# A staggered start of attention, and VectorE's preparation ahead of a wait

## The reference

```
h = token_mixer(x)                       # conv, layer norm, feed forward, max-pool: 748 rows remain
h = h + recurrence(layernorm(h))
h = h + experts_2_of_8(layernorm(h))     # routed, plus a shared one
n = layernorm(h)
q, k, v = n @ W_qkv + b                  # 8 heads of 16
q', k' = relu(q), relu(k), each times cos and times sin of the position
h = h + (causal linear attention of q', k', v) @ W_out + b_out
n = layernorm(h)                         # for the last, routed layer:
logits = conv3(gelu(conv3(n)));  shared = conv1(silu(conv9(n)))
h = h + layernorm(n + experts_2_of_10(n, logits) + shared)
```

## Time and profile before

| | us |
|---|---|
| median of 3 runs | 1531.79 |
| lowest and highest | 1531.74, 1535.3 |
| the profiled execution | 1544.43 |
| its span, first to last instruction | 1542.6 |
| busy in it: PE, VectorE, ScalarE, GpSimd | 1305.9, 1003.6, 644.9, 699.3 |
| mean granted PE clock, as a share of 2.4 GHz | 0.92 |

### The profile page before, as it was taken

How to read it: one execution, slowest core, us unless ns; L and a number is a source line. 1 busy time by engine, 2 the same in 40 slices (tenths; PEclk the granted TensorE clock), 3 DMA queues, 4 the chain that set the end, 5 groups by cost and what they waited for, 6 DMA issues and landing times.

```text
span 1542.6 us, 33397 instructions
## 1 busy us (share of the span) xinstructions
PE 1305.9 (85%) x10360; PEld 1103.2 (72%) x10361; DVE 1003.6 (65%) x3235; ACT 644.9 (42%) x1610; POOL 699.3 (45%) x1055
## 2 busy tenths in 40 slices
PE   6696777787899937778899899988998989999974
PEld 3464646564899935556788778876887989999953
DVE  4467768665466656757863786467663628989946
ACT  1346272523122204335335453445334436666623
POOL 0112556444688853133531444242614526777732
PEclk9697989898999978989999899999998999999987
DMA  6000400003588840010010001000100237777725
GB/s 191 4 21 6 111 27 22 25 21 95 161 266 256 263 170 1 2 42 1 24 61 0 2 14 58 14 1 1 43 1 8 95 97 191 196 194 198 196 88 161
DMA packets 102202, 128.46 MB, mean 83 GB/s; under 512 B 21015, under 2 KB 61181, under 8 KB 101842
## 3 DMA queue, kind: packets, MB, share of 16 engines
q1 hardware_dynamic: 88786, 102.36, 23.1%
q0 software_dynamic: 13312, 24.74, 4.8%
HBM read 96.13 MB, written 34.94 MB: 85 GB/s over the span
## 4 chain that ended last, share of the span: by engine, by line
PE 60%; DVE 15%; issue 7%; DVEq 6%; POOL 5%; ACT 4%; DMA 2%; POOLq 0%; SPq 0%; ACTq 0%
PE psum L980 12%; PE psum L1133 11%; PE psum L989 9%; DVE work L1554 3%; PE psum L1142 3%; PE psum L1047 2%; POOL rows_in L2130 2%; PE psum L1094 2%; PE psum L1072 2%; PE psum L794 2%; PE psum L1191 2%; PE psum L969 2%; PE psum L1018 2%; DVE stats L1537 2%; PE psum L1067 1%
## 5 line engine op out<-in xcount | busy, mean ns | idle before, releaser
L1133 PE MATMUL psum<-NT,wreg 128*128 128x182 f32 (+1 forms) x1536 | 261.6, 326 | 10.2 <-ACT pack L1434 5.1
L1133 PEld LDWEIGHTS psum<-NT,wreg 128*128 128x128 f32 x1536 | 247.9, 192 | 18.9 <-ACT pack L1434 5.9
L2162 POOL DMA_INDIRECT rows_out<-work,expert_row_kept x208 | 206.2, 992 | 79.6 <-issue 41.1
L980 PE MATMUL psum<-work 128*128 128x128 f32 x1664 | 222.7, 277 | 0.9 <-ACT work L1336 0.9
L980 PEld LDWEIGHTS psum<-work 128*128 128x128 f32 x1664 | 203.9, 193 | 1.7 <-issue 0.9
L2111 POOL TENSOR_TENSOR rstd<-var_eps,pack 128x6 f32<-128x6 f32 x40 | 56.5, 1415 | 215.0 <-DVE var_eps L1544 214.9
L1329 ACT ACTIVATE work<-psum,work 128x128 f32<-128x128 f32 x416 | 118.6, 368 | 64.4 <-PE psum L980 64.3
L1876 DVE SCALAR_TENSOR_TENSOR work<-psum,work 128x128 f32<-128x128 f32 x416 | 117.1, 344 | 7.7
L794 PE MATMUL psum<-pack,work 128*128 128x128 f32 (+2 forms) x288 | 51.4, 336 | 82.0 <-DVE work L1554 75.5
L1885 DVE TENSOR_SCALAR work<-psum,expert_row_kept 128x128 f32<-128x128 f32 x208 | 72.8, 350 | 71.8 <-PE psum L969 36.6
L2130 POOL DMA_INDIRECT rows_in<-N,slot_now x96 | 100.5, 1046 | 28.6 <-issue 28.4
(11 more groups left out here) (364 smaller groups left out, 2894.3 us busy)
## 6 DMA issues: line engine op xcount, KB each, us to landing
work<-w_and_b SPq DMA_DIRECT2D x104, 258.0 KB
work<-in_ew SPq DMA_DIRECT2D x104, 256.0 KB
work<-rows_in SPq DMA_DIRECT2D x208, 65.0 KB
work<-rows_out SPq DMA_DIRECT2D x32, 384.0 KB, 4.2
rows_out<-work,expert_row_kept POOLq DMA_INDIRECT x208
work<-in_xT SPq DMA_DIRECT2D x8, 375.0 KB, 3.0
w_and_b<-in_ew SPq DMA_DIRECT2D x1, 2560.0 KB
out<-H SPq DMA_DIRECT2D x8, 320.0 KB
```

What stands on the lines that cost most here:

```text
L980: r_ = mm(v.ps1[:, c * P:(c + 1) * P], v.w1[:, c * P:(c + 1) * P], v.xT, start=True, stop=True)
L1133: r = mm(bank[:, half * HALF_PAIRS:half * HALF_PAIRS + p1 - p0], weights[:, m * P:(m + 1) * P], product_input(name, g, k, p0, p1), start=( ...
L2162: G.indirect_dma_start(rows_out[m], bass.IndirectOffsetOnAxis(ap=v.dest, axis=0), v.y, None, bounds_check=last, oob_is_err=False).then_inc ...
```

## The change

There are three edits. In `interleaved`, when no convolution parts are mixed in (the first pass), the steps ahead of the chunks are sorted so that lane 1 is one step behind lane 0 from step 2 on. On VectorE the preparation of tap weights and routing values stands ahead of its wait for the stores; clearing the value tiles stays behind it. And on VectorE the norm of lane 1 moves from step 2 to step 1, right behind its variance, in all four passes.

```diff
         def interleaved(conv):
             order, n, reached = [], 0, 0
-            for x in range(ATT_STEPS * LANES):
-                order.append(("attention", x // LANES, x % LANES))
-                reached += FILL[x // LANES]
+            turns_ = [(x // LANES, x % LANES) for x in range(ATT_STEPS * LANES)]
+            if not conv:
+                ahead = [x for x in turns_ if x[0] < CHUNKS]
+                ahead.sort(key=lambda x: (x[0] + (x[1] if x[0] > 1 else 0), x[1]))
+                turns_ = ahead + turns_[len(ahead):]
+            for step, lane_ in turns_:
+                order.append(("attention", step, lane_))
+                reached += FILL[step]
...
             barrier(e, "experts0")
-            for s in row_stored:
-                e.wait_ge(s, 16 * RITERS)
-            for v in lanes:
-                V.memset(v.V[:, :, :, 0:3 * DH], 0.0)
-                V.memset(v.V[:, :, :, 3 * DH:], 1.0)
             V.memset(rc2_taps, 0.0)
...
             V.tensor_tensor(tap_sum, tap_sum, w("ident")[0:96, 64:64 + E1], ALU.add)
             e.drain()
+            e.wait_ge(row_bias_in, 16)
+            route_begin, onehot, values, take, slots_, *_ = route(1, False)
+            route_begin()
...
+            for s in row_stored:
+                e.wait_ge(s, 16 * RITERS)
+            for v in lanes:
+                V.memset(v.V[:, :, :, 0:3 * DH], 0.0)
+                V.memset(v.V[:, :, :, 3 * DH:], 1.0)
...
             def second_step(k, i):
-                (norm5 if k == 0 else var5)(k, i)
-
-            def third_step(k, i):
                 if k > 0:
-                    norm5(k, i)
-
-            att = {0: [begin_lane], 1: [second_step], 2: [third_step]}
+                    var5(k, i)
+                norm5(k, i)
+
+            att = {0: [begin_lane], 1: [second_step]}
```

More of the change, by code:

```diff
@@ L1903, in _ @@
             e.drain()
+            e.wait_ge(row_bias_in, 16)
+            route_begin, onehot, values, take, slots_, *_ = route(1, False)
+            route_begin()
+            _, onehot_last, values_last, take_last, slots_last, _, tables_count, tables_expert, tables_row = route(1)
+            for s in row_stored:
[3 more added lines that the diff above has]
+                V.memset(v.V[:, :, :, 3 * DH:], 1.0)
             def sum_rows(v, i, k, phase):
@@ L1973, in add_attention @@
                 e.drain().then_inc(dve_done[k], dve.step("attention", "h4", k))
[L1975 to L1978, removed]
             var5, norm5 = var(5, "attention", Hb, WIDTH), norm(5, "attention", Hb, WIDTH)
```

## The result

The changed kernel takes 1546.5 us (median of 4, 1542.7 to 1549.3), the kernel before 1532.2 us in the same comparison (1531.7 to 1535.3): a ratio of 1.0087, 95% interval 1.0061 to 1.0114. It is slower by 13 us (9 to 17), where 9.5 us were forecast. The profiled execution of the changed kernel took 1545.4 us (span 1543.5), about its median.

What follows compares the result with a forecast made beforehand. The chain was taken as 60% TensorE and 15% VectorE, most of the rest gaps. Terms 4.5 + 3.0 + 3.0 - 0.7 - 0.3 = +9.5 us on 1531.8 gave 1541.3 us, range 1534.5 to 1545.5.

Steps and rivals of the forecast that it cites:

- The moved preparation: Entry into attention: VectorE's preparation goes into its idle wait, so lane 0's sum starts earlier; gain 0.7 us.
- The first pass: First pass: q0 of lane 0 fills PE's gap, 1.55 us, but ScalarE is late next; gain 0.3 us.
- The lag of q0 in the loop: Loop passes: combination behind lane 1's norm delays silu, the copy and q0, by 3.3, 3.0 and 3.0 us.
- GpSimd's hold: Loop passes: GpSimd's bias addition of lane 1 stretches an operation of VectorE's combination by 1.34 us, within q0's lag.
- The clock: First loop pass: PE idles longer before q0, its granted clock falls to 0.50; 1.25 us more.
- (a): Loop rival: small lag, GpSimd doesn't hold the combination and the clock stays up; +4.2 us, 1536.0 us; chance 0.17.
- (b): Loop rival: no lag, other ScalarE or PE work sets q0 and hides the late silu; 1530.8 us; chance 0.08.
- (c): First-pass rival: the stagger pays 5.6 us by early clock and weight additions, against 5.2 lag; 1531.4 us; chance 0.06.
- (d): Loop rival: slow clock takes the second projection too, in all three passes; +13.2 us, 1545.0 us; chance 0.17.

Runs made afterwards that it cites:

- run 8: Kernel before with only the moved preparation, a single execution: 3.95 us from VectorE's wake-up to its sum, where it was 4.55.
- run 1: Kernel before with only lane 1's norm moved right behind its variance, in all passes; ratio 1.0067 to the kernel before.
- run 9: Changed kernel with ten idle matmuls on PE behind each lane's transposes in the loop; ratio 1.0029 to the kernel before.
- run 2: Changed kernel with lane 1's norm moved in the first pass alone, the loop's as before; ratio 0.9978 to the kernel before.
- run 3: Changed kernel with ScalarE's silu put behind the copies of both lanes' transposes in the loop; ratio 1.0009 to the kernel before.
- Run 4: Changed kernel with GpSimd adding lane 1's output bias behind lane 0's value bias in the loop; ratio 1.0031 to the kernel before.
- run 5: The changed kernel again, unaltered, on another chip; ratio 1.0061 to the kernel before.
- run 7: From run 2, the stagger in the loop too, lane 1's norm behind the convolution part; ratio 1.0014 to the kernel before.
- run 10: From run 2, in the loop only q0 of lane 0 put ahead of lane 1's transposes, norm placed as in run 7; 1529.3 us, ratio 0.9956.

## Why the forecast was right

- **The moved preparation, 0.7 us.** It was 0.67 in the changed kernel and 0.60 in run 8. The limit named, the landing of lane 0's rows, is what releases the sum now. The 0.1 us put down for VectorE's reaction was an estimate; in the changed kernel the load landed at 562.59 and the sum began at 562.61. Stores issued later, with VectorE at work beside GpSimd, would have taken gain away; the changed kernel and run 8 show no delay in their issue. The last store's DMA took 5.74 us in the earlier trace rows and 5.77 in the changed kernel, both times while SP's load of the convolution weights was under way, 8.6 us from issue to landing. The moved instructions are short, 0.36 us for three copies in run 8, and no run tries long ones.
- **The first pass, 0.3 us: not shown.** The mechanism is seen: q0 runs in the gap, and lane 1's value projection then waits 1.66 us for ScalarE (592.42). The size is not. Up to lane 1's first scores the changed kernel took 0.4 us less than before, but the nine runs with this order took 33.1 to 34.5 us, and the three with the order of before (the kernel before, runs 1 and 8) 33.1, 33.8 and 33.8. That it came near the forecast in the changed kernel is luck. One thing that scatters is when the clock comes back: 18.4 us after the sum in the changed kernel, 20.5 in run 9, the same order on all engines, with first scores at 33.4 and 34.4:

```profile
581.00:582.00 1.00, 1.00 (x5) 0.62 (x4) 0.00 (x0) 0.48 (x2) 0.00 (x0) 0.97 0.00 0
```

```profile
582.00:583.00 1.00, 1.00 (x3) 0.42 (x2) 0.00 (x0) 0.97 (x2) 0.00 (x0) 0.50 0.00 0
583.00:584.00 1.00, 1.00 (x4) 0.63 (x3) 0.94 (x1) 0.02 (x1) 0.00 (x0) 0.85 0.00 0
```

- **The lag of q0 in the loop.** Forecast 3.3, 3.0 and 3.0 us; measured 3.19, 2.91 and 3.03. Runs 1 to 3 show the cause: only this edit, only in the loop, and only through silu's place ahead of the copy.
- **GpSimd's hold, 1.34 of it.** It was 1.43, in two parts: the third operation took 1.54 us instead of 0.36, and the fourth 0.60 (872.60) instead of the 0.35 of the earlier trace rows. Run 4, which moves the addition, took 1.43 us off the lag. The third operation ended soon after the addition did: GpSimd's addition over 128x640 ran 1.72 us from 870.74, to 872.46, and the third operation, started at 871.14, ended at 872.68. The hold is not one-sided: GpSimd's two additions took 2.25 us beside the combination and 1.95 in the earlier trace rows.
- **The clock, 1.25 us in the first loop pass.** From sum to count that pass lost 4.69, forecast 4.5. Run 9 gives the term by itself: with PE kept busy (granted clock 1.00 against 0.50) and the same lag of q0, the first relu comes 1.34 us sooner after q0's start, and sum to count takes 4.0 us less over three passes. That is also more than I had put in: in the second and third pass too, q0 was slow before (2.54 us in both the earlier trace rows) and is slow now (2.91 us to the first relu in both, 874.63 to 877.54 and 1044.31 to 1047.22, at a granted clock of 0.50), so idle matmuls gain there against both.
- **Sum.** Up to the counts the forecast was 10.5 and the changed kernel shows 11.05, run 1 12.9 and run 5 12.5 against run 2. The whole times say 13 us (9 to 17) in the first comparison and 10 us (5 to 15) in run 5; 9.5 lies in both, in the first at its very edge. The median is 5 us over the forecast one, and nothing in the stages that the runs resolve accounts for that difference.
- **The rivals.** (a), without hold and fall of the clock, and (b), without lag, are excluded by the rows above and by runs 4 and 9; (c) needed (b). (d), a slow second projection in all three passes, would give 1545.0 us, nearer to the median of 1546.5 than the forecast. The traces speak against it all the same: the clock is back about when q0 ends, and relu to count is unchanged in passes 1 and 2. In the third pass 0.14 us of it can be seen. The chances were added a little wrong: by their own terms slower comes to 0.75 and faster to 0.07.

## What to carry to other kernels

An instruction that waits may have work ahead of it that costs nothing; before moving the waiting instruction forward, look up what was hidden in the wait and who waits for that, in every queue and every pass that the code serves, not only in the one it was written for. Where a late result hurts, look at the order in the consumer's queue: moving the instruction that waits behind two copies that don't (run 3) gave back all but 0.6 us of what the move had cost. And a stagger of whole chains can lose behind what it gains in front (run 7), where moving the one step that fills the pause (run 10) kept its gain, if a smaller one.

## What the runs showed of the hardware

The pause ahead of q0 cost PE twice here. In the changed kernel's first loop pass PE stood idle for 3.18 us, and q0's matmuls then ran at a granted clock of 0.50 (2.90 us to the first relu); with ten idle matmuls in the pause they ran at 1.00 (1.56 us), started as late behind the norm. And each of the idle float32 matmuls is two matmul records in the trace (the ten behind a lane's transposes are x20 and take 2.41 us), so the cost of a record, 0.12 us, is half the cost of such a matmul. The four matmuls of a projection, as they are counted above, are two instructions of the program; the transposes, x6 for six tiles, are one record each.
